# Routing logits with the router weights stationary, and scores and combine weights transposed on VectorE in 32x32 blocks

## Chip, cores and metric

One Trainium2 chip, one core. The metric is the device time of one launch in microseconds (us). Of the kernel before, three runs were timed: 956.42, 960.41 and 960.45 us, median 960.41 us.

## What is computed

Eight rows of 512 tokens with 128 channels go through three layers, each with a residual: a mixture-of-experts feed-forward layer (FFN) at half weight, a Mamba layer, and the same FFN again with the same weights.

```
x = x + 0.5 * ffn(layernorm(x)); x = x + mamba(layernorm(x)); x = x + 0.5 * ffn(layernorm(x))

logits = x @ router_w.T                      # 16 experts
scores = sigmoid(logits); s = scores + bias
group_score = top_k(s in 4 groups of 4, 2).sum; the best 2 groups stay, others are masked
topk_idx = top_k(masked, 4); tw = scores at topk_idx; tw = tw / tw.sum * 2.5
combine = one_hot(topk_idx) * tw             # tokens x 16, mostly zeros
y[e] = (silu(x @ gate_w[e]) * (x @ up_w[e])) @ down_w[e]
ffn = sum over e of y[e] * combine[:, e]  + the same with 2 shared experts, weight 1
```

Everything is float32. The Mamba layer projects, runs a short convolution and a GELU, forms delta, B and C, and scans 16 states per channel over 512 steps.

## The kernel before

The kernel is written for all five engines by hand, in three stages that overlap at their ends: the first FFN (object f1), the Mamba layer, the second FFN (object f2). Each engine has its own generator; the order of instructions on an engine is the order of the yields, and semaphores join the engines.

**The FFN in blocks.** A block is one expert (or one of the 2 shared ones, which come first) of one row of 512 tokens: 18 blocks a row, 144 a layer, numbered g. The float32 products are made of three single-pass products of rounded parts (high x high, low x high, high x low): TensorE issues in each block three matmuls for h (lines L1004, L1005, L1008), three for u (the same lines) and three for the down product of the block four earlier (L986, L987, L988), each 512 columns. ScalarE computes silu(h) (L711, shared experts L701), VectorE multiplies it by the combine weight (L904) and by u (L910), ScalarE rounds the result (L720) and GpSimd subtracts to get the low part (L616). The weight that L904 multiplies by is one expert's combine weight of 512 tokens, the same in all 128 partitions: SyncE loads it from DRAM with a broadcasting DMA into one of 8 slots of `c_ring` (L575). For the first two experts of f1's row 0, TensorE spreads it into PSUM instead (`pe_spread_first`, L971).

**Routing.** For rows in pairs (in f1 rows 0 and 1 singly) the work goes: normalised x is transposed by TensorE (L489) and copied to `xt` (L632); TensorE forms the logits (`pe_logits`, L953), with the tokens of a tile as the stationary operand and the router's 16 columns as the moving one, so that they land with tokens in partitions; ScalarE makes scores from them (`act_scores`, L644, L647); VectorE selects (`dve_route`, L774 to L850) in 13 pieces, one or two in a block; TensorE transposes the combine weights, four tiles a row (`pe_transpose_comb`, L962), into the PSUM half-bank `misc`; ScalarE copies 16 x 512 out of it (`act_copy_ct`, L654); SyncE stores them to DRAM with one DMA (`store_row`, L566), and loads each expert's row back by broadcast. What happens at which block is in the tables `SLOW` and `QUICK` (the second for f1's rows 2 and 3 alone): the step after a pair's start at which x is normalised, turned, copied, the logits and scores are made, the route's pieces, and the turns and copies of the combine weights.

```python
SLOW = Prep((6, 7), (8, 10), (9, 11), 13, 14, {15 + n: 1 for n in range(13)}, (30, 32), (31, 33))
QUICK = Prep((5, 6), (7, 9), (8, 10), 12, 13, {14 + n: 2 for n in range(7)}, (23, 25), (24, 26))
PAIRED = {2: 9, 4: 37, 6: 73}, {2: 1, 4: 37, 6: 73}
```

f1's row 0 is routed before the first block, its row 1 in the blocks 6 to 13. f2's rows 0 and 1 are routed in the last part of the Mamba stage, between the scans; the tables `FRONT_DVE`, `FRONT_PE` and `FRONT_ACT` say after which pair of states. While row 0 of either layer is routed, many operands of VectorE lie in PSUM (`scratch`).

**The Mamba stage** goes by 64 half-rows ("pairs": two states of a row). TensorE spreads B into PSUM (L1462), VectorE multiplies (L1381) and scans (L1411), GpSimd multiplies by C (L1188), TensorE adds the states up (L1474); at the end of each row it projects with plain float32 matmuls (L1484, L1485) and VectorE adds to x (L1395).

**SyncE's queue** issues in order: x, weights, the small operands of the Mamba layer (L319), then the stores of combine weights and the loads of `c_ring`, each load after its slot is free, and at a row's start after that row's store has landed.

## Time and profile before

| | us |
|---|---|
| profiled execution, its own time | 958.39 |
| its span | 956.7 |
| median of 3 runs (lowest, highest) | 960.41 (956.42, 960.45) |
| TensorE busy | 899.6 |
| VectorE busy | 733.7 |
| GpSimd busy | 644.1 |
| ScalarE busy | 582.3 |

TensorE's mean granted clock is 0.987 of full speed. f1 reaches to about 320 us of the span, the Mamba stage to about 635, f2 to the end. Matmul records overlap (each begins before the last one's end), so what a matmul costs is read from one start to the next.

### The profile page before, as it was taken

The numbers are of one execution on the slowest core, as the hardware profiler recorded it, in microseconds if no ns is written. First come the engines' busy times: TensorE is split into PE (matmuls) and PEld (weight loads), VectorE is DVE, ScalarE is ACT, GpSimd is POOL, SyncE is SP. The second block draws the span as 40 slices with busy tenths as digits, with TensorE's granted clock in tenths as the row PEclk, the third lists the DMA queues.
The fourth block names the chain that finished last, engine by engine and source line by source line (L and its number), as shares of the span: only waits on it lengthen the run. The fifth ranks groups of instructions, "written<-read, shape, count | busy, mean of one in ns | idle before, by whom it ended". The sixth has DMA issues, their size and how long they took to land. (4 is left out here: it accounts for less than half of the span.)

```text
span 956.7 us, 11995 instructions
## 1 busy us (share of the span) xinstructions
PE 899.6 (94%) x3623; PEld 641.1 (67%) x3623; DVE 733.7 (77%) x1223; ACT 582.3 (61%) x1038; POOL 644.1 (67%) x469
## 2 busy tenths in 40 slices
PE   5888999999999999899999978799999999999997
PEld 4566788788876766444445424368878878888885
DVE  4777777876874568999999999956877787695664
ACT  5454565566564677889767785226557556555554
POOL 6556575666654465999999888546667567565665
PEclk9999999999999999999999999799999999999999
DMA  9522232243232223344433443233333225334430
GB/s 253 163 77 96 92 120 93 72 150 113 91 101 84 83 77 101 111 156 154 148 133 127 148 151 114 89 127 115 112 104 128 93 87 158 102 99 128 136 113 13
DMA packets 62001, 110.31 MB, mean 115 GB/s; under 512 B 7400, under 2 KB 19824, under 8 KB 61936
## 3 DMA queue, kind: packets, MB, share of 16 engines
q1 hardware_dynamic: 61936, 109.54, 35.6%
q8 instruction: 29, 0.48, 0.2%
q14 instruction: 36, 0.29, 0.1%
HBM read 106.63 MB, written 2.88 MB: 114 GB/s over the span
## 5 line engine op out<-in xcount | busy, mean ns | idle before, releaser
L616 POOL TENSOR_TENSOR act_lo<-act,act_hi 128x512 fp32r<-128x512 f32 x288 | 375.5, 1305 | 263.4 <-ACT act_hi L720 262.8
L711 ACT ACTIVATE bank<-bank 128x512 f32<-128x512 f32 x254 | 147.7, 582 | 250.6 <-PE bank L1008 235.1
L904 DVE TENSOR_TENSOR sg<-bank,c_ring 128x512 f32<-128x512 f32 x254 | 174.2, 686 | 124.1 <-ACT bank L711 118.3
L1004 PE MATMUL bank<-x_parts,w_hi 128*128 128x512 f32 x576 | 241.6, 419 | 14.2 <-DVE act L910 12.5
L910 DVE TENSOR_TENSOR act<-sg,bank 128x512 f32<-128x512 f32 x288 | 198.1, 688 | 59.5 <-PE bank L1008 29.7
L1008 PE MATMUL bank<-x_parts,w_hi 128*128 128x512 f32 x576 | 229.3, 398 | 0.0
L1005 PE MATMUL bank<-x_parts,w_lo 128*128 128x512 f32 x576 | 229.1, 398 | 0.0
L720 ACT ACTIVATE act_hi<-act 128x512 fp32r<-128x512 f32 x288 | 179.4, 623 | 1.7 <-DVE act L910 1.0
L1004 PEld LDWEIGHTS bank<-x_parts,w_hi 128*128 128x128 f32 x576 | 109.7, 191 | 51.0 <-DVE act L910 22.8
L1008 PEld LDWEIGHTS bank<-x_parts,w_hi 128*128 128x128 f32 x576 | 109.6, 190 | 25.9
L1005 PEld LDWEIGHTS bank<-x_parts,w_lo 128*128 128x128 f32 x576 | 110.2, 191 | 24.1 <-issue 2.6
L986 PE MATMUL bank<-act_hi,w_hi 128*128 128x512 f32 x288 | 115.0, 399 | 2.6 <-POOL act_lo L616 2.6
L1275 ACT ACTIVATE stage<-delta,a_neg 128x511 f32<-128x511 f32 x128 | 83.5, 711 | 55.2 <-POOL delta L1158 35.1
L988 PE MATMUL bank<-act_lo,w_hi 128*128 128x512 f32 x288 | 114.0, 396 | 0.0
L987 PE MATMUL bank<-act_hi,w_lo 128*128 128x512 f32 x288 | 113.7, 395 | 0.0
L1188 POOL TENSOR_TENSOR stage<-stage,c_ring 128x1024 f32<-128x1024 f32 x32 | 75.5, 2366 | 14.9 <-DVE stage L1411 14.8
L1188 POOL TENSOR_TENSOR states<-states,c_ring 128x1024 f32<-128x1024 f32 x32 | 75.7, 2367 | 11.9 <-DVE states L1411 11.9
L1381 DVE TENSOR_TENSOR bank<-du,bank 128x1024 f32<-128x1024 f32 x64 | 77.2, 1207 | 3.7 <-PE bank L1462 3.5
L1411 DVE TENSOR_TENSOR_SCAN states<-stage,bank 128x1024 f32<-128x1024 f32 x32 | 73.1, 2283 | 2.2
L1411 DVE TENSOR_TENSOR_SCAN stage<-stage,bank 128x1024 f32<-128x1024 f32 x32 | 72.9, 2278 | 1.1
L1462 PE MATMUL bank<-bc_parts,sel_n 128*128 128x512 f32 x128 | 56.0, 519 | 14.2 <-DVE stage L1411 10.8
L1474 PE MATMUL bank<-states,ident 128*128 128x512 f32 x128 | 63.8, 624 | 4.1 <-DVE y_sb L1389 4.1
(173 smaller groups left out, 1056.4 us busy)
## 6 DMA issues: line engine op xcount, KB each, us to landing
c_ring<-c_dram SPq DMA_DIRECT2D x254, 256.0 KB, 3.2
c_ring<-c_dram SPq DMA_DIRECT2D x64, 512.0 KB, 3.7
out<-x_sb SPq DMA_DIRECT2D x8, 256.0 KB, 2.6
stage<-in_L_ffn_gate_w SPq DMA_DIRECT2D x4, 256.0 KB, 4.9
stage<-in_L_ffn_up_w SPq DMA_DIRECT2D x4, 256.0 KB, 5.1
stage<-in_L_ffn_down_w SPq DMA_DIRECT2D x4, 256.0 KB, 5.2
c_dram<-c_rows SPq DMA_DIRECT2D x24, 32.0 KB, 3.2
x_sb<-in_L_attn_hidden_states SPq DMA_DIRECT2D x2, 256.0 KB, 2.9
```

The costliest lines, as they stand in the source:

```text
L616: self.nc.gpsimd.tensor_tensor(m["act_lo"][:, g % LAG], m["act"][:, g % ACTS], m["act_hi"][:, g % LAG].bitcast(FP32), ALU.subtract).then_i ...
L711: nc.scalar.activation(self.s_bank[:, g % 2], self.h_bank[:, g % 2], ACT.Silu).then_inc(self.sg_ready, 1)
L720: nc.scalar.activation(m["act_hi"][:, j % LAG], m["act"][:, j % ACTS], ACT.Copy).then_inc(self.hi_ready, 1)
L904: nc.vector.tensor_tensor(m["sg"][:, g % 2], silu, weight, ALU.mult).then_inc(self.w_done, 1)
L910: nc.vector.tensor_tensor(m["act"][:, g % ACTS], m["sg"][:, g % 2], self.u_bank[:, g % 2], ALU.mult).then_inc(self.act_ready, 1)
L986: nc.tensor.matmul(self.acc, hi, m["act_hi"][:, j % LAG], start=first, stop=False, skip_group_check=True)
L988: nc.tensor.matmul(self.acc, hi, m["act_lo"][:, j % LAG], start=False, stop=last, skip_group_check=True).then_inc(self.down_done, 1)
L1004: nc.tensor.matmul(dst, m["w_hi"][:, k, n, :], x_hi, start=True, stop=False)
L1005: nc.tensor.matmul(dst, m["w_lo"][:, k, n, :], x_hi, start=False, stop=False)
L1008: return nc.tensor.matmul(dst, m["w_hi"][:, k, n, :], x_lo, start=False, stop=True)
L1188: nc.gpsimd.tensor_tensor(self.state(g), self.state(g), m["c_ring"][:, 2 * (n % RING):2 * (n % RING) + 2], ALU.mult).then_inc(self.mul_don ...
L1411: nc.vector.tensor_tensor_scan(flat(self.state(g)), flat(self.decay[:, g % RING]), flat(self.b_bank[g % 2][:]), 0.0, ALU.mult, ALU.add).th ...
```

## The change

1. The router's weights become the stationary operand (padded with zeros to 32 columns) and 128 tokens the moving one. Each of a row's four tiles of tokens goes to its own 32 partitions of PSUM, which is its own group of 32 columns of TensorE's array. The logits land with experts in partitions: tile t in partitions 32t to 32t+15.
2. ScalarE's two score operations run over 128 x 256 for a pair of rows, not 128 x 128, and write `score_rows` in SBUF.
3. VectorE transposes that in 32x32 blocks into `score` (or the PSUM scratch for row 0), where each tile has 32 places of which 16 are used; and at the end of the route, in a piece of its own, it transposes `comb` (now 32 wide, zeroed at the start) into `c_rows`.
4. TensorE's transposes of the combine weights and ScalarE's copies of them are gone.
5. `c_rows` has tile t in partitions 32t to 32t+15, so a row is stored by four DMAs of 16 x 128, not one of 16 x 512. The Mamba stage gets its own buffer `bc_rows`, and two waits that kept the shared one apart are gone.
6. The first spread reads the new layout: 8 matmuls of 128 columns with 128 partitions, in place of 2 of 512 with 16, one block earlier.

Each object's operations for the parts 1 to 5, cut to the core:

```diff
-FRONT_DVE = {41: 1, 43: 1, 45: 1, 54: 2, 55: 2, 56: 2, 57: 2, 58: 2, 59: 1, 60: 1, 61: 1}
+FRONT_DVE = {41: 1, 43: 1, 45: 1, 54: 2, 55: 2, 56: 2, 57: 2, 58: 2, 59: 1, 60: 1, 61: 1, 62: 1}
-FRONT_ACT = (46, 48, 50, 52, 54, 56, 62)
-FRONT_PE = (49, 51, 52, 61)
+FRONT_ACT = (46, 48, 50, 52, 54, 56)
+FRONT_PE = (49, 51, 52)
-SLOW = Prep((6, 7), (8, 10), (9, 11), 13, 14, {15 + n: 1 for n in range(13)}, (30, 32), (31, 33))
-QUICK = Prep((5, 6), (7, 9), (8, 10), 12, 13, {14 + n: 2 for n in range(7)}, (23, 25), (24, 26))
+SLOW = Prep((6, 7), (8, 10), (9, 11), 13, 14, {15 + n: 1 for n in range(14)})
+QUICK = Prep((5, 6), (7, 9), (8, 10), 12, 13, {14 + n: 2 for n in range(7)})
...
         def store_row(r):
-            sp.wait_ge(self.ct_copied, r + 1)
-            sp.dma_start(self.c_dram[r], m["c_rows"][0:E, r % 2, :]).then_inc(self.ct_stored, 16)
+            sp.wait_ge(self.ct_turned, r + 1)
+            for t in range(TT):
+                sp.dma_start(c_parts[r, t], m["c_rows"][t * Q:t * Q + E, r % 2]).then_inc(self.ct_stored, 16)
...
-    def act_copy_ct(self, ae, r):
...
         dve.wait_ge(self.score_ready, b + 1)
+        cols = slice(P * (r % 2), P * (r % 2 + rows))
+        nc.vector.transpose(turned.rearrange("p t e -> p (t e)"), m["score_rows"][:].rearrange("p r k -> p (r k)")[:, cols]
+                            ).then_inc(self.turned, 1)
+        dve.wait_ge(self.turned, b + 1)
...
+        yield
+        dve.wait_ge(self.comb_ready, b + 1)
+        for n in range(r, r + rows):
+            need(dve, self.ct_stored, self.STORED * (n - 1))
+            nc.vector.transpose(m["c_rows"][:, n % 2], m["comb"][:, TT * (n % 2):TT * (n % 2 + 1)].rearrange(
+                "p t e -> p (t e)")).then_inc(self.ct_turned, 1)
         yield
...
                 if self.p == 0 and 6 <= g < 14:
                     next(routing, None)
-                    if g < 10:
+                    if g < 11:
                         next(routing, None)
...
         for n in range(rows * TT):
-            q, t = (r + n // TT) % 2, n % TT
-            last = nc.tensor.matmul(self.misc[:, n * E:(n + 1) * E], m["xt"][:, q, t * P:(t + 1) * P],
-                                    m["router_sb"][:, :], start=True, stop=True)
+            q, t = n // TT, n % TT
+            last = nc.tensor.matmul(self.misc[t * Q:(t + 1) * Q, q * P:(q + 1) * P], m["router_sb"][:, :],
+                                    m["xt"][:, (r + q) % 2, t * P:(t + 1) * P], start=True, stop=True)
...
-    def pe_transpose_comb(self, pe, r):
```

On TensorE, in f2 at the turn of row 2's combine weights (L962 is that group of four; L988 and L1004 are the block's matmuls around it). Before:

```order
L986 MATMUL bank<-act_hi,w_hi 128x512
L987 MATMUL bank<-act_hi,w_lo 128x512
L988 MATMUL bank<-act_lo,w_hi 128x512
L962 MATMUL bank<-ident,comb 16x128 x4
L1004 MATMUL bank<-x_parts,w_hi 128x512
L1005 MATMUL bank<-x_parts,w_lo 128x512
```

Changed, the same place (the lines have moved up by one):

```order
L985 MATMUL bank<-act_hi,w_hi 128x512
L986 MATMUL bank<-act_hi,w_lo 128x512
L987 MATMUL bank<-act_lo,w_hi 128x512
L1003 MATMUL bank<-x_parts,w_hi 128x512
L1004 MATMUL bank<-x_parts,w_lo 128x512
```

The group of four is gone there and at the other 15 rows of the two layers; the group of logits stays where it was (`L953 ... 128x16 x8` has become `L958 ... 32x128 x8`).

On VectorE, at the end of the Mamba stage, the last three scans (L1411, in the changed kernel L1400; L850 and L849 write the combine weights). Before:

```order
L850 SCALAR_TENSOR_TENSOR comb<-bank,total 128x128
L1411 SCALAR_TENSOR_TENSOR stage<-stage,bank 128x1024
L1381 TENSOR_TENSOR bank<-du,bank 128x1024
L1411 SCALAR_TENSOR_TENSOR stage<-stage,bank 128x1024
L910 TENSOR_TENSOR act<-sg,bank 128x512 x2
```

Changed:

```order
L849 SCALAR_TENSOR_TENSOR comb<-bank,total 128x8x16
L1400 SCALAR_TENSOR_TENSOR stage<-stage,bank 128x1024
L1370 TENSOR_TENSOR bank<-du,bank 128x1024
L856 STREAM_TRANSPOSE c_rows<-comb 128x128 x2
L1400 SCALAR_TENSOR_TENSOR stage<-stage,bank 128x1024
L915 TENSOR_TENSOR act<-sg,bank 128x512 x2
```

Two transposes now stand ahead of the stage's last scan.

On SyncE's queue, at f1's row 0, before and changed:

```order
L319 DMA a_log_sb<-in_L_attn_A_log 128x16
L566 DMA c_dram<-c_rows 16x512
L575 DMA c_ring<-c_dram 128x512 x14
L566 DMA c_dram<-c_rows 16x512
L575 DMA c_ring<-c_dram 128x512 x16
```

```order
L322 DMA a_log_sb<-in_L_attn_A_log 128x16
L575 DMA c_dram<-c_rows 16x128 x4
L584 DMA c_ring<-c_dram 128x512 x14
L575 DMA c_dram<-c_rows 16x128 x4
L584 DMA c_ring<-c_dram 128x512 x16
```

Each store of a row is four issues in place of one, and stands at the same place among the loads.

## Rows read from the trace of the kernel before

**Rows 1.** The page's first part: busy time by engine.
```profile
PE 899.6 (94%) x3623; PEld 641.1 (67%) x3623; DVE 733.7 (77%) x1223; ACT 582.3 (61%) x1038; POOL 644.1 (67%) x469
```
**Rows 2.** Stages: length, busy time of PE, PEld, DVE, ACT, POOL, clock, DMA.
```profile
31.30:60.00 28.70, 21.79 (x83) 15.60 (x84) 27.35 (x68) 12.25 (x20) 16.60 (x12) 0.94 0.33 108
...
84.00:108.00 24.00, 19.48 (x75) 14.47 (x74) 22.79 (x48) 9.86 (x18) 14.70 (x15) 0.93 0.15 47
108.00:240.00 132.00, 132.00 (x609) 106.95 (x607) 95.00 (x189) 79.44 (x154) 83.89 (x66) 1.00 0.34 113
...
582.00:624.00 42.00, 32.73 (x83) 15.44 (x82) 41.40 (x58) 13.34 (x21) 27.38 (x14) 0.84 0.30 107
...
640.00:945.00 305.00, 305.00 (x1377) 247.17 (x1376) 221.59 (x416) 178.84 (x335) 194.55 (x153) 1.00 0.35 111
```
**Rows 3.** Timeline of PE, f1: a turn of combine weights (start, length).
```profile
112.54 0.40 PE L988 MATMUL bank<-act_lo,w_hi 128*128 128x512 f32 x1
112.77 0.60 PE L962 MATMUL bank<-ident,comb 128*16 128x128 f32 x4
113.13 0.48 PE L1004 MATMUL bank<-x_parts,w_hi 128*128 128x512 f32 x1
113.44 0.39 PE L1005 MATMUL bank<-x_parts,w_lo 128*128 128x512 f32 x1
```
**Rows 4.** Timeline of PE, f2: a pair's logits.
```profile
663.73 1.85 PE L953 MATMUL bank<-router_sb,xt 128*128 128x16 f32 x16
665.43 0.48 PE L1004 MATMUL bank<-x_parts,w_hi 128*128 128x512 f32 x1
665.75 0.39 PE L1005 MATMUL bank<-x_parts,w_lo 128*128 128x512 f32 x1
```
**Rows 5.** Timeline of PE, Mamba stage: float32 matmuls of 128 moving columns.
```profile
612.37 0.38 PE L1484 MATMUL bank<-w_out_sb,y_sb 128*128 128x128 f32 x2
612.59 0.39 PE L1485 MATMUL bank<-w_out_sb,z 128*128 128x128 f32 x2
```
**Rows 6.** Groups of DVE by form: busy us, mean ns of one, idle before.
```profile
L787 DVE TENSOR_REDUCE g_score<-pair_sum 128x32 f32<-128x192 f32 x7 | 2.4, 349 | 0.1
...
L803 DVE TENSOR_REDUCE g_rank<-g_ge 128x32 f32<-128x128 f32 x6 | 1.7, 280 | 0.0
...
L774 DVE TENSOR_TENSOR biased<-score,bias_sb 128x64 f32<-128x64 f32 x1 | 1.2, 1232 | 0.0
...
L774 DVE TENSOR_TENSOR biased<-bank,bias_sb 128x64 f32<-128x64 f32 x1 | 0.2, 209 | 0.0
```
**Rows 7.** Timeline of SP, f1's first store and the loads behind it.
```profile
25.56 0.43 SPq L319 DMA_DIRECT2D a_log_sb<-in_L_attn_A_log  x1
26.03 0.43 SPq L566 DMA_DIRECT2D c_dram<-c_rows  x1
28.05 1.28 SPq L575 DMA_DIRECT2D c_ring<-c_dram  x3
```
**Rows 8.** Timeline of DVE, f1: the first product with a loaded weight.
```profile
31.27 0.69 DVE L904 TENSOR_TENSOR sg<-bank,c_ring 128x512 f32<-128x512 f32 x1 [4.46 <-DMA c_ring<-c_dram]
```
**Rows 9.** Timeline of PE, f1: the turn of row 1's combine weights.
```profile
59.38 0.60 PE L962 MATMUL bank<-ident,comb 128*16 128x128 f32 x4 [0.57 <-DVE comb L850]
```
**Rows 10.** Timeline of DVE and POOL, Mamba stage: after the logits, and the last scan.
```profile
581.31 1.23 DVE L1381 TENSOR_TENSOR bank<-du,bank 128x1024 f32<-128x1024 f32 x1 [1.53 <-PE bank L1462]
...
621.05 2.35 POOL L1188 TENSOR_TENSOR stage<-stage,c_ring 128x1024 f32<-128x1024 f32 x1 [1.99 <-DVE stage L1411]
...
622.12 2.29 DVE L1411 TENSOR_TENSOR_SCAN stage<-stage,bank 128x1024 f32<-128x1024 f32 x1
```
**Rows 11.** Waits from 640 to 920 us: total us, times, longest.
```profile
PEld bank L1004 <- DVE act L910: 1.6, 6, 0.3
```

More of the change, by code:

```diff
@@ L16 @@
 TT = SEQ // P
+Q = 32
 E, NSH = 16, 2
@@ L103, in program @@
         c2_dram = nc.dram_tensor("c2_dram", (BATCH, NS, SEQ), FP32, kind="Internal").ap()
-        th = sb("th", [P, 2 * TT, E])
-        score = sb("score", [P, 2 * TT, E])
+        th = sb("th", [P, 2, P])
+        score_rows = sb("score_rows", [P, 2, P])
+        score = sb("score", [P, 2 * TT, Q])
         biased = sb("biased", [P, 2 * TT, E])
@@ L490, in pe_transpose @@
         last.then_inc(self.xt_ready, 1)
-Prep = namedtuple("Prep", "apply turn copy logits scores route comb_turn comb_copy")
-SLOW = Prep((6, 7), (8, 10), (9, 11), 13, 14, {15 + n: 1 for n in range(13)}, (30, 32), (31, 33))
-QUICK = Prep((5, 6), (7, 9), (8, 10), 12, 13, {14 + n: 2 for n in range(7)}, (23, 25), (24, 26))
+Prep = namedtuple("Prep", "apply turn copy logits scores route")
+SLOW = Prep((6, 7), (8, 10), (9, 11), 13, 14, {15 + n: 1 for n in range(14)})
+QUICK = Prep((5, 6), (7, 9), (8, 10), 12, 13, {14 + n: 2 for n in range(7)})
 class Ffn:
     FIRST_STEPS, ROUTE_STEPS = 27, 25
+    STORED = 16 * P // Q
     PAIRED = {2: 9, 4: 37, 6: 73}, {2: 1, 4: 37, 6: 73}
@@ L758, in dve_route @@
         g_rank, g_in = m["g_rank"][:, 0:nt * GROUPS], m["g_in"][:, 0:nt * GROUPS]
-        score, comb = self.route_score(r, rows), m["comb"][:, tiles]
+        turned, comb = self.route_score(r, rows), m["comb"][:, tiles, 0:E]
+        score = turned[:, :, 0:E]
+        g_rank = g_rank.rearrange("p (t g) -> p t g", t=nt)
         if r == 0:
             part = lambda n: self.scratch[:, n * nt * E:(n + 1) * nt * E].rearrange("p (t e) -> p t e", t=nt)
-            rest = lambda n: self.scratch[:, 3 * nt * E:3 * nt * E + nt * n]
-            biased_too = masked = part(1)
-            g_ge = part(2).rearrange("p t (g h) -> p t g h", g=GROUPS)
-            tied = part(2)
-            g_rank, total_too = rest(GROUPS), self.scratch[:, 2 * nt * E:2 * nt * E + nt]
-            g_score_too, n_above, weighted = rest(GROUPS).rearrange("p (t g) -> p t g", t=nt), rest(1), part(3)
+            biased_too = masked = weighted = part(2)
+            g_ge = part(3).rearrange("p t (g h) -> p t g h", g=GROUPS)
+            tied = part(3)
+            total_too = self.scratch[:, 3 * nt * E:3 * nt * E + nt]
+            g_score_too = g_rank = turned[:, :, E:E + GROUPS]
+            n_above = turned[:, :, E]
         else:
@@ L951, in pe_logits @@
         for n in range(rows * TT):
-            q, t = (r + n // TT) % 2, n % TT
-            last = nc.tensor.matmul(self.misc[:, n * E:(n + 1) * E], m["xt"][:, q, t * P:(t + 1) * P],
-                                    m["router_sb"][:, :], start=True, stop=True)
+            q, t = n // TT, n % TT
+            last = nc.tensor.matmul(self.misc[t * Q:(t + 1) * Q, q * P:(q + 1) * P], m["router_sb"][:, :],
+                                    m["xt"][:, (r + q) % 2, t * P:(t + 1) * P], start=True, stop=True)
         last.then_inc(self.logits_ready, 1)
-    def pe_transpose_comb(self, pe, r):
-        nc, m = self.nc, self.m
-        self.onto_misc(pe, self.ct_copied, r + 1)
-        pe.wait_ge(self.comb_ready, self.rows_before(r) + 1)
-        for t in range(TT):
-            last = nc.tensor.transpose(self.misc[0:E, t * P:(t + 1) * P], m["comb"][:, TT * (r % 2) + t, :],
-                                       m["ident"][:, :])
-        last.then_inc(self.ct_ready, 1)
     def pe_spread_first(self, pe):
         self.onto_misc(pe, self.w_done, 1)
-        pe.wait_ge(self.ct_copied, 1)
+        pe.wait_ge(self.ct_turned, 1)
         for e, dst in enumerate((self.misc, self.acc)):
-            self.nc.tensor.matmul(dst, self.m["ident"][0:E, e:e + 1].broadcast_to([E, P]),
-                                  self.m["c_rows"][0:E, 0, :], start=True, stop=True).then_inc(self.spread_ready, 1)
+            for t in range(TT):
+                last = self.nc.tensor.matmul(dst[:, t * P:(t + 1) * P],
+                                             self.m["ident"][:, t * Q + e:t * Q + e + 1].broadcast_to([P, P]),
+                                             self.m["c_rows"][:, 0], start=True, stop=True)
+            last.then_inc(self.spread_ready, 1)
     def pe_down(self, pe, j):
```

67 lines of the change are left out of this document (23 added, 44 removed).

## The prediction, made before the changed kernel was run

> **What bounds the kernel now.** I read the page's busy times first [rows 1]: TensorE is busy for 94% of the span, no other engine above 77%. Such a share is a mean over stages, so I read the table by stage next [rows 2], and it splits the kernel in two kinds of ground. In f2 from 640 to 945 us, and in f1 from 108 to 240 us, TensorE is busy for every microsecond: there each thing taken off its queue shortens the run, and VectorE, busy for about 72% of the time, has room. In f1 from 31 to 60 and from 84 to 108 us, and at the end of the Mamba stage, 582 to 624 us, VectorE is busy for 95% or more and TensorE waits: there TensorE's savings are worth nothing, and each thing put on VectorE lengthens the run. The change takes from TensorE and gives to VectorE, so its parts have to be sorted by stage. The timelines then give the price of each. The sum below is made against the profiled execution's 958.39 us; that is 2.0 us under the median of 960.41, so I put the same difference on the median.
>
> **TensorE: turns of combine weights.** A group of four transposes stands between a block's last down matmul and the next h [rows 3]. Without it, L1004 would start 0.23 us after L988 at 112.77, and L1005 0.23 us later at 113.00; it starts at 113.44. So a group costs 0.44 us, of which about 0.09 is that the matmul behind it starts its successor late (0.31, not 0.23, from 113.13 to 113.44). There are 16 groups. Two are ahead of or at the first blocks of a layer where TensorE waits for others anyway (row 0 of each), f2's row 1 is followed by a wait for VectorE, and f1's row 1 lies in VectorE's stretch. The other 12 lie on TensorE's full ground: 12 x 0.44 = **5.3 us off**.
>
> **TensorE: logits.** The 8 matmuls of a pair are 16 half-products, and the group costs, counted the same way, 665.75 - 663.73 - 0.23 = 1.79 us [rows 4]; 16 x 0.106 and 0.09 behind. Now each moves 128 columns, not 16. The nearest row is the Mamba stage's float32 projection, 128 moving columns: two halves from 612.37 to 612.59, 0.11 us each [rows 5]. No row of the trace shows matmuls on different column groups, so the price must be bounded. If they run one behind the other, 16 x 0.11 + 0.09 = 1.85: nothing gained. If all four tiles of a row run side by side, 4 x 0.11 + 0.09 = 0.53. I take what lies between, for a reason in the order: the two halves of one matmul stand next to each other and use the same column group, so they must follow each other; a half can run beside the next tile's first half only. That gives 9 steps in place of 16: 9 x 0.11 + 0.09 = 1.08. Changing the array from one partition to four and back I charge with 0.2 a group, twice the 0.09 to 0.1 that the trace shows behind a switch between float32 and rounded matmuls [rows 3, 4]. That leaves 1.79 - 1.28 = 0.5 us gained a group, with -0.3 (serial, 1.85 + 0.2) and +1.1 (0.53 + 0.2) as ends. On full ground there are 6 groups, three in each layer; the seventh, for f2's first pair, has VectorE waiting 1.53 us behind it for a spread matmul queued after the logits [rows 10], so it counts too: 7 x 0.5 = **3.5 us off**, ends +1.8 and -7.4.
> The Trainium skill (TensorE: Matmul & The Clock Gate, Part 3) says that matmuls on different column groups start about 4 ns apart, and (TensorEngine Tiling, Key Properties) that changing the tiling mode drains the engine. By the first alone the time would be the side-by-side case; the second speaks against the change and would take some of it back. No row here shows either.
>
> **VectorE: transposes.** 9 for scores, 16 for combine weights. Each reads one SBUF tensor and has no row; the nearest are reductions with one input: 128 elements 280 ns, 192 elements 349 ns [rows 6], so 0.28 for 128 and 0.42 for 256. Where TensorE is full they cost nothing, as long as VectorE does not fall behind by more than it is ahead: between 640 and 920 us TensorE's weight loads waited for it for 1.6 us in six places [rows 11], and the transposes come one or two to a block of 2.1 us in which VectorE is busy for 1.5. If that cover were gone, six pairs times 0.98 us (0.42 + 2 x 0.28) would be exposed. Where VectorE is the bound:
> - 31 to 60 us, row 1's route: 0.28 + 0.28 = 0.56 more. In return TensorE no longer stops at the turn of row 1's weights, for which it waits 0.57 us [rows 9] and then spends 0.44. The acts behind it are as late as VectorE, so I count back only the 0.44: **+0.1** (ends -0.5 and +0.6).
> - 84 to 108 us, rows 2 and 3 at two pieces a block: 0.42 + 0.56, **+1.0**.
> - the Mamba stage's end: 0.42 before the first piece, 0.56 directly ahead of the last scan at 622.12 [rows 10], which GpSimd, the last sums and f2's first block wait for: **+1.0**.
> ScalarE's 16 copies (out of a queue busy 61%) and its two wider score operations change nothing; they have idle time beside them at all places. What follows the transposes in SyncE's queue is now ready sooner than before, except at f2's start, where the first loaded weight is used 15 us later.
>
> **SyncE: four stores for one.** Each issue takes 0.47 us from one start to the next [rows 7]. In the steady part the stores stand well ahead of their use and nothing waits. At f1's row 0 they do not: SyncE is busy with small operands up to 26.03, the loads of `c_ring` start when the store has landed at 28.05, and VectorE waits 4.46 us for the first of them [rows 8], with TensorE behind it. Three more issues put all of that back: 3 x 0.47 = **+1.4**. All else at f1's start (the spread a block earlier, row 0's route 0.56 longer) ends before that load and is hidden by this wait.
>
> **Sum.** -5.3 - 3.5 + 0.1 + 1.0 + 1.0 + 1.4 = -5.3 us: 953.1 against the profiled execution, **955.1 us** against the median. About 0.5%, 4.8 us, is what a measurement of this kernel can tell from no change.
>
> **Rivals.**
> - *Column groups one behind the other.* For it: the names say only where results land, and no row shows an overlap of float32 halves. Then the logits lose 0.3 a group: -5.3 + 1.8 + 3.5 = 0.0, 960.4 us. The whole of the change is then the transposes against VectorE and SyncE. In this case the logits group would cost about 2.0 us in the profile.
> - *All four tiles side by side.* -5.3 - 7.4 + 3.5 = -9.2, 951.2 us. Against it: the halves of a tile are neighbours in the queue.
> - *The transposes wait for GpSimd (slower).* The trace has VectorE operations that last 1.23 us, not 0.21, when both inputs are in SBUF [rows 6]: they start while GpSimd works. If the transposes are held in the same way, each costs up to 1.0 us more in f1's two VectorE stretches (5 of them) and up to 2.35 - 0.28 = 2.1 us in the Mamba stage, where GpSimd's operation of 2.35 us starts at 621.05, just when the two new ones stand ahead of the last scan [rows 10] (3 of them). -5.3 + 5.0 + 6.3 = +6.0: 966.4 us. It ends slower than before from 10.1 us of such waiting upward (5.3 to cancel the gain and 4.8 over it), some 90% of what is possible. Against it: reductions, with one input, show no such spread. The Trainium skill (SBUF — State Buffer, Who interferes with whom) says that only VectorE instructions with two SBUF inputs or in a two-port mode contend with GpSimd; by that rule this rival falls, and the rows of the reductions agree.
> - *A dearer switch.* If draining costs 0.5 us more a group than charged, 3.5 us come back: 958.6.
>
> **Chances.** The forecast's case, column groups that overlap in part and free transposes: 0.47, with some 1.5 us on either side. Serial groups (with the dearer switch): 0.26. Side by side: 0.14. Held transposes, wholly or in part: 0.10. Something not seen: 0.03. The forecast lies just beyond the 0.5% bound, so a little over half of its case, 0.27, counts as faster; with side by side and a rest, 0.44. Within 0.5%: the other 0.20, 0.21 of serial, a little of held transposes, 0.43. Slower: 0.13, most of it from the held transposes and the rest from a switch or a drain dearer than the trace can show. The range takes in the three cases without the held transposes' end, and the bounds of the small terms: 950.0 to 962.5.
>
> **What would show it.** The gap that the logits leave on TensorE, from the group's start to the second matmul behind it: 1.5 us in the forecast (0.23 more than the group's cost), 2.3 serial, 1.0 side by side. L1004 straight behind L988 at the old turns. Transposes of 0.28 and 0.42 us, with no long ones. VectorE's wait for the first `c_ring` load grown, and that load landing 1.4 us later; the last scan 1 us later against the start of the route. If f2's full stretch, first h of row 1 to last down product, is not 4 us shorter (6 turns x 0.44 + 3 x 0.5), the TensorE half is wrong; if it is and the total is not, the price was paid in f1.

## The result, and the profile after

The changed kernel takes **947.49 us** (median of 4 runs, 945.70 to 948.37) against 960.12 for the kernel before (4 runs, 956.42 to 960.45). The ratio is 0.988 with a 95% interval of 0.9855 to 0.9905: faster by 1.2%, some 12.6 us. The forecast was 955.1, the range 950.0 to 962.5: the time lies below the range, past even the rival with the best end (all tiles side by side, 951.2). The profiled execution took 948.37 us, span 946.5, against 958.39 and 956.7 before.

The page's first part, as [rows 1], and the table by stage, as [rows 2]; the stages from the Mamba layer's end on now start 6 us earlier (start and end in the first column, the length behind them, then as in [rows 2]).

```profile
PE 885.0 (93%) x3571; PEld 622.9 (66%) x3571; DVE 735.2 (78%) x1249; ACT 576.4 (61%) x1022; POOL 643.6 (68%) x470
```

```profile
34.00:62.00 28.00, 22.16 (x77) 16.16 (x78) 26.27 (x68) 12.16 (x20) 15.11 (x11) 0.88 0.36 113
86.00:108.00 22.00, 18.39 (x73) 12.90 (x72) 20.74 (x49) 9.15 (x16) 14.78 (x16) 1.00 0.17 50
108.00:240.00 132.00, 132.00 (x607) 105.31 (x606) 98.31 (x199) 79.92 (x153) 85.40 (x68) 1.00 0.37 113
576.00:618.00 42.00, 32.04 (x101) 15.20 (x101) 40.67 (x59) 12.95 (x20) 26.80 (x14) 0.92 0.31 100
634.00:935.00 301.00, 301.00 (x1355) 240.89 (x1354) 223.97 (x429) 177.02 (x330) 195.33 (x154) 1.00 0.36 112
```

The kinds of ground are the same: TensorE still full in f2 and late f1, VectorE still the bound in the two early stretches and at the Mamba stage's end. VectorE's total rose by 1.5 us only (733.7 to 735.2) although the 25 transposes bring 7.7 us of work: some of its old work became shorter. That is the first hint of what the forecast missed.

Where the time went is best read between fixed points: the start of ScalarE's silu of a block, and of VectorE's last long scan. Differences of the two profiled executions, with what the forecast's own terms put into each stretch:

| Stretch | before | after | difference | forecast |
|---|---|---|---|---|
| span's start to f1 block 6 | 32.05 | 35.10 | +3.05 | +1.4 |
| f1 block 6 to 36 (both VectorE stretches, 1 logits, 2 turns of pairs) | 84.14 | 79.52 | -4.62 | -0.3 |
| f1 block 36 to 110 (2 logits, 4 turns) | 167.08 | 163.92 | -3.16 | -2.8 |
| f1 block 110 to the last scan | 338.85 | 340.61 | +1.76 | +0.5 |
| last scan to f2 block 3 | 17.22 | 14.69 | -2.53 | 0 |
| f2 block 3 to 143 (3 logits, 6 turns) | 306.48 | 301.84 | -4.64 | -4.1 |
| sum | | | -10.14 | -5.3 |

**Logits.** TensorE's timeline at the place of [rows 4], then at that of [rows 3] (start, length).

```profile
658.09 0.39 PE L987 MATMUL bank<-act_lo,w_hi 128*128 128x512 f32 x1
658.41 0.64 PE L958 MATMUL bank<-xt,router_sb 128*32 128x128 f32 x16
658.99 0.50 PE L1003 MATMUL bank<-x_parts,w_hi 128*128 128x512 f32 x1
659.32 0.40 PE L1004 MATMUL bank<-x_parts,w_lo 128*128 128x512 f32 x1
```

```profile
111.39 0.39 PE L987 MATMUL bank<-act_lo,w_hi 128*128 128x512 f32 x1
111.62 0.40 PE L1003 MATMUL bank<-x_parts,w_hi 128*128 128x512 f32 x1
111.86 0.39 PE L1004 MATMUL bank<-x_parts,w_lo 128*128 128x512 f32 x1
```

From L987 to L1004 it is 1.23 us with the logits between, and 0.47 without: a group of logits costs 0.76 us, where it cost 1.78 counted the same way. That is 1.02 gained a group, twice the 0.5 of the forecast. The single records show why: the sixteen halves start in four rounds of four, 0.11 to 0.13 us from round to round and 6 to 7 ns from one half to the next within a round. From the group's start to the second matmul behind it the gap is 0.91: of the three markers (1.5, 2.3, 1.0) the side-by-side one. The turn has left no trace: L1003 stands straight behind L987.

**The start of f1.** Timeline of SyncE, then of VectorE, as [rows 7] and [rows 8].

```profile
26.04 0.43 SPq L322 DMA_DIRECT2D a_log_sb<-in_L_attn_A_log  x1
26.51 1.82 SPq L575 DMA_DIRECT2D c_dram<-c_rows  x4
30.80 0.34 SPq L584 DMA_DIRECT2D c_ring<-c_dram  x1
```

```profile
34.31 0.69 DVE L909 TENSOR_TENSOR sg<-bank,c_ring 128x512 f32<-128x512 f32 x1 [7.87 <-DMA c_ring<-c_dram]
```

From the first store's issue to the first load's it is now 4.29 us, before 2.02: 1.4 of the growth are the three more issues, 0.9 is that the last of the four took 2.87 us from issue to landing (the first three 1.75 to 1.87), the single one 2.00. With the queue 0.48 us later already at the store (26.51, not 26.03) and the load itself 0.29 us slower (30.80 to 34.31, before 28.05 to 31.27), VectorE's wait ends 3.04 us later.

**The transposes.** VectorE's groups by form.

```profile
L856 DVE STREAM_TRANSPOSE c_rows<-comb 128x128 f32<-128x128 f32 x16 | 4.1, 290 | 0.1
L771 DVE STREAM_TRANSPOSE score<-score_rows 128x256 f32<-128x256 f32 x6 | 2.6, 438 | 0.0
...
L771 DVE STREAM_TRANSPOSE score<-score_rows 128x128 f32<-128x128 f32 x1 | 0.3, 303 | 0.0
```

0.29 and 0.44 us against 0.28 and 0.42 estimated. The longest of all 25 took 0.45, though 23 of them ran, at least in part, while a GpSimd operation did: the slower rival, transposes held by GpSimd, is out. (The rule cited for it, the Trainium skill, SBUF — State Buffer, Who interferes with whom, agrees.)

### The profile page after: what moved, and what is told of

It is laid out like the page before. It is cut to its first block and busy times, and to the rows that moved or that the text cites. A ratio compares the mean times of both kernels' runs of the same rounds, so it can differ in the third digit from the quotient of the medians.

```text
span 946.5 us, 11926 instructions
## 1 busy us (share of the span) xinstructions
PE 885.0 (93%) x3571; PEld 622.9 (66%) x3571; DVE 735.2 (78%) x1249; ACT 576.4 (61%) x1022; POOL 643.6 (68%) x470
## 5 line engine op out<-in xcount | busy, mean ns | idle before, releaser
L1003 PE MATMUL bank<-x_parts,w_hi 128*128 128x512 f32 x576 | 240.3, 417 | 19.6 <-DVE act L915 16.0
L1004 PE MATMUL bank<-x_parts,w_lo 128*128 128x512 f32 x576 | 229.2, 398 | 0.0
L1003 PEld LDWEIGHTS bank<-x_parts,w_hi 128*128 128x128 f32 x576 | 109.1, 189 | 59.1 <-DVE act L915 26.5
L1004 PEld LDWEIGHTS bank<-x_parts,w_lo 128*128 128x128 f32 x576 | 109.3, 190 | 25.2 <-issue 2.6
L987 PE MATMUL bank<-act_lo,w_hi 128*128 128x512 f32 x288 | 114.3, 397 | 0.0
L1400 DVE TENSOR_TENSOR_SCAN states<-stage,bank 128x1024 f32<-128x1024 f32 x32 | 73.0, 2282 | 3.9 <-PE bank L1463 1.9
L1400 DVE TENSOR_TENSOR_SCAN stage<-stage,bank 128x1024 f32<-128x1024 f32 x32 | 72.9, 2278 | 1.0
L1463 PE MATMUL bank<-states,ident 128*128 128x512 f32 x128 | 66.7, 648 | 4.6 <-DVE y_sb L1378 4.6
```

Source lines behind the costliest of these rows:

```text
L1003: nc.tensor.matmul(dst, m["w_hi"][:, k, n, :], x_hi, start=True, stop=False)
L1004: nc.tensor.matmul(dst, m["w_lo"][:, k, n, :], x_hi, start=False, stop=False)
L1400: nc.vector.tensor_tensor_scan(flat(self.state(g)), flat(self.decay[:, g % RING]), flat(self.b_bank[g % 2][:]), 0.0, ALU.mult, ALU.add).th ...
```

## The experiments

Twelve kernels ran, four at a time on one chip with the kernel before. The intervals are those of the ratio to it; its median was 960.10 us beside the first four, 960.59 beside the second four, and 958.79 beside the last four, which ran on another chip. So times of the last four are compared with the others' by their ratios. "f1's block 6 to 36" and the like are stretches read as in the table above.

### The changed kernel again

> The changed kernel once more, unchanged, as the yardstick of this series and for a second trace. If what happened in the first layer's VectorE-bound stretches belongs to the program, the block of f1 that comes 3.05 us late at g = 6 comes 3 us late again, and the lead at the second layer's start is again about 5 us. If it was the luck of one execution, these two numbers move by 1 us or more. Time 947.5.

**947.00 us**, ratio 0.9867 (0.984 to 0.9895). Block 6 of f1 came at 35.10 again, exactly; block 36 at 114.52 (114.62 in the first trace). The lead at f2's first block was 7.3 us, where the first trace had 5.8: f1's block 110 to the last scan took 339.27, not 340.61. So in these two executions the start and f1's lengths repeat, and the Mamba stage scatters. In four traces of kernels that leave this stage as it was before, it takes 338.85, 342.97, 341.09 and 340.16 us. The first of these is that of the kernel before: its profiled execution had the shortest Mamba stage of all, which is part of why the profiled executions differ by 10.0 us and the medians by 12.6.

### One column group, two column groups

```diff
-            last = nc.tensor.matmul(self.misc[t * Q:(t + 1) * Q, q * P:(q + 1) * P], ...
+            last = nc.tensor.matmul(self.misc[0:Q, q * P:(q + 1) * P], ...
```

> All tiles of tokens put their logits on the first column group, one over the other (so the scores are those of the last tile of a row, and three quarters of the score rows hold what was there before). Same instructions, same sizes, only the column group differs. Theory A, the four groups run side by side: on one group the 16 halves follow each other at 0.11 us, a group of logits costs about 1.9 us instead of 0.77, and on the six groups that TensorE's queue decides this gives 6 x 1.1 = 6.7 us back: about 954. Theory B, a matmul with 32 stationary columns is cheap by itself, wherever its result lands: the gap stays at 1.0 us from the group's start to the second matmul behind it, and the time at 947.5.

```diff
+            last = nc.tensor.matmul(self.misc[(t % 2) * Q:(t % 2 + 1) * Q, q * P:(q + 1) * P], ...
```

> Tiles alternate between the first two column groups (the scores of two of the four tiles are overwritten, half of the score rows hold what was there before). Theory A, neighbours on different groups overlap: eight steps of 0.11 instead of about four, a group of logits costs 1.2 to 1.3 us, the time is about 950.5. If instead two halves of one matmul must follow each other and only neighbours overlap (the forecast's reason), two groups are as good as four, and the time stays at 947.5. Theory B: 947.5 as well, so this run counts together with the one on a single group.

One group: **956.52 us**, ratio 0.996 (0.9943 to 0.9977). Two groups: **950.59**, ratio 0.9904 (0.9877 to 0.9931). Timelines of TensorE at the same logits of f2, first with one group, then with two.

```profile
661.83 0.39 PE L987 MATMUL bank<-act_lo,w_hi 128*128 128x512 f32 x1
662.15 1.93 PE L958 MATMUL bank<-xt,router_sb 128*32 128x128 f32 x16
664.01 0.51 PE L1003 MATMUL bank<-x_parts,w_hi 128*128 128x512 f32 x1
664.36 0.39 PE L1004 MATMUL bank<-x_parts,w_lo 128*128 128x512 f32 x1
```

```profile
659.76 0.39 PE L987 MATMUL bank<-act_lo,w_hi 128*128 128x512 f32 x1
660.08 1.07 PE L958 MATMUL bank<-xt,router_sb 128*32 128x128 f32 x16
661.08 0.51 PE L1003 MATMUL bank<-x_parts,w_hi 128*128 128x512 f32 x1
661.42 0.39 PE L1004 MATMUL bank<-x_parts,w_lo 128*128 128x512 f32 x1
```

Counted as above (L987 to L1004 less 0.47) a group costs 2.06 us with one column group, 1.19 with two, 0.76 with four. The three lie on a line: one group to two saves 0.87 = 8 x 0.109, two to four saves 0.43 = 4 x 0.108. So the 16 halves go in 16, 8 and 4 rounds of 0.11 us, and 0.33 us is left over that does not depend on the groups. The forecast had charged 0.29 for the change of the array's shape and the slower start behind it; that these are what the 0.33 pays for fits, but no run changes the shape alone. Theory A is shown, and the forecast's reason is not only weakened but excluded: if two halves of one matmul held up the queue, two groups would be as good as four. The single-group kernel also confirms the serial case of the forecast, 1.85 + 0.2 = 2.05 a group. Its time is 9.5 us over that of the changed kernel beside it, where 6.7 was expected: 7 x 1.30 = 9.1, which fits all seven groups counting, the one in the Mamba stage too. (The Trainium skill, TensorE: Matmul & The Clock Gate, Part 3, has it that matmuls on different column groups start about 4 ns apart. The traces agree in kind: the halves of four tiles start 6 to 7 ns apart and run at the same time, in float32 too.)

### The turns alone

Router and scores as before, the combine weights turned by VectorE and stored four times. The old logits put tokens on other partitions than the turn by blocks assumes, so the weights belong to other tokens of the row; amount and order of the work are those described.

```diff
-            last = nc.tensor.matmul(self.misc[t * Q:(t + 1) * Q, q * P:(q + 1) * P], m["router_sb"][:, :],
-                                    m["xt"][:, (r + q) % 2, t * P:(t + 1) * P], start=True, stop=True)
+            last = nc.tensor.matmul(self.misc[:, n * E:(n + 1) * E], m["xt"][:, (r + q) % 2, t * P:(t + 1) * P],
+                                    m["router_sb"][:, 0:E], start=True, stop=True)
...
-        nc.vector.transpose(turned.rearrange("p t e -> p (t e)"), ...
```

> The combine weights turned by VectorE as in the change, with the four stores, but logits and scores as before: tokens stationary, 16 moving columns, no transpose of scores. If the logits' part is worth 6 x 1.0 us on TensorE's full ground and its extra transposes cost nothing, this run is 6 us slower than the changed kernel: 953.5. If the better VectorE stretches of f1 came with the logits' part, it is slower still, 955 to 957. The late start must show in both cases: block g = 6 of f1 about 3 us late, since the stores are in it.

**954.30 us**, ratio 0.995 (0.9928 to 0.9973): the turns, with the late start that they bring, are worth 5.8 us, the logits with their scores the other 7.3, near to 7 x 1.02. In f1's blocks 18 to 24, where one group of logits stands, this kernel takes 15.26 us, the changed one 14.24: there too the whole 1.02 is gained. Each turn takes 0.40 to 0.43 us out of f2's blocks (forecast 0.44), and block 6 of f1 is late by 3.19 us: the late start is in the stores, as expected.

### GpSimd's subtraction cut short, in both kernels

```diff
+                w = 8 if self.p == 0 and 5 <= g < 60 else SEQ
-                self.nc.gpsimd.tensor_tensor(m["act_lo"][:, g % LAG], m["act"][:, g % ACTS], ...
+                self.nc.gpsimd.tensor_tensor(m["act_lo"][:, g % LAG, 0:w], m["act"][:, g % ACTS, 0:w], ...
```

> The kernel before, with GpSimd's subtraction act_lo cut from 512 to 8 columns in f1's blocks 5 to 59 (the low part of these acts is then stale, so the output is off in the last bits). Theory A, f1's VectorE-bound stretches are long because small VectorE operations with two inputs wait for this 1.29 us subtraction: before has ten such operations there, 6.5 to 9 us more than they need, so this kernel is 5 to 9 us faster than the kernel before, 951 to 955, and without long small operations in the two stretches. Theory B, the collisions are hidden by other waits: no more than 1 us faster.

> The same cut in the changed kernel. Theory A, the change was better than forecast in f1's VectorE stretches only because it met GpSimd less often there (2.1 us of it in two operations of rows 2 and 3): with the collisions gone in both kernels, block 28 of f1 relative to before is no longer 4.7 us (3.7 without the logits' gain) ahead of where block 6 stood, but behind by the transposes' own time, about 1 us, less the gains of TensorE; after gains only 3 to 5 us from the cut, and the gap between the kernels closes from 13 to 9 or 10 us. Theory B, the gain there comes from TensorE's turns being gone: the gap stays at 13.

What is suspected, in the rows. Kernel before, timeline of VectorE and under it of GpSimd, 88 to 99 us (an operation's start and length):

```profile
88.52 1.43 DVE L800 TENSOR_TENSOR g_ge<-g_ge,g_gt 128x128 f32<-128x128 f32 x1
...
97.62 1.42 DVE L831 TENSOR_TENSOR tie_at<-tie_at,n_above 128x128 f32<-128x128 f32 x1
```

```profile
88.51 1.29 POOL L616 TENSOR_TENSOR act_lo<-act,act_hi 128x512 fp32r<-128x512 f32 x1 [0.33 <-ACT act_hi L720]
...
97.59 1.29 POOL L616 TENSOR_TENSOR act_lo<-act,act_hi 128x512 fp32r<-128x512 f32 x1 [2.58 <-ACT act_hi L720]
```

The changed kernel, the same two operations and the GpSimd subtraction beside them:

```profile
89.51 0.29 DVE L800 TENSOR_TENSOR g_ge<-g_ge,g_gt 128x128 f32<-128x128 f32 x1
98.11 0.29 DVE L831 TENSOR_TENSOR tie_at<-tie_at,n_above 128x128 f32<-128x128 f32 x1
```

```profile
89.53 1.43 POOL L625 TENSOR_TENSOR act_lo<-act,act_hi 128x512 fp32r<-128x512 f32 x1 [0.33 <-ACT act_hi L718]
...
98.61 1.29 POOL L625 TENSOR_TENSOR act_lo<-act,act_hi 128x512 fp32r<-128x512 f32 x1 [0.81 <-ACT act_hi L718]
```

Before, VectorE's L800 starts 0.01 us behind GpSimd's subtraction and needs 1.43 us; after, it starts 0.02 us ahead of it, needs 0.29, and GpSimd's takes 1.43 in place of 1.29. Who comes second waits, and if that is a VectorE operation of 0.3 us, it waits for up to 1.15. The kernel before has ten small VectorE operations of routes and norm drawn out to 0.8 us or more in the two stretches, 11.6 us together; the changed one has six, 6.6 us together.

Measured: the kernel before with the cut **952.12 us**, ratio 0.992 (0.9899 to 0.994), the changed one with the cut **942.66**, ratio 0.982 (0.9789 to 0.985). Against 960.59 and the changed kernel's 947.49, the cut gains 8.5 us in the kernel before and 4.8 in the changed one, and the gap closes from 13.1 to 9.5. The cut also ends GpSimd's own work sooner, but TensorE waited only once for that work in f1's block 6 to 36 before, 0.2 us, and not at all in the changed kernel: what is gained is the collisions. In the traces f1's block 6 to 36 falls from 84.14 to 76.43 before, and from 79.52 to 74.44 after: without most collisions (two long operations are left before, one after) the change gains 1.99 us in this stretch, with them 4.62. Theory A holds; in these traces 2.6 us of the result are collisions that fell better. Which part of the change moved VectorE against GpSimd so (the late start, the transposes, the turns gone from TensorE) is not separated.

The other traces say where this is luck. L800 and L831 in f1's blocks 24 to 36 are held in the trace of the kernel before and in that of the same kernel with the early store (33.06 and 33.13 us for these blocks), and not in that of the kernel before shifted by 64 bytes (31.11; both kernels come below). All traces with the change and the full subtraction take 30.45 to 30.50 there but one, the combined kernel: it holds both again and takes 32.31. So three quarters of the gain in blocks 24 to 36 (1.95 of 2.57 us) hang on an order of events that small changes undo.

### The start: one store, and an early store

One store of all 128 partitions a row, in place of four:

```diff
-            for t in range(TT):
-                sp.dma_start(c_parts[r, t], m["c_rows"][t * Q:t * Q + E, r % 2]).then_inc(self.ct_stored, 16)
+            sp.dma_start(c_parts[r], m["c_rows"][:, r % 2]).then_inc(self.ct_stored, 16)
```

> A row's weights stored with one DMA from all 128 partitions (rows of unused experts too, into a DRAM tensor twice as tall) in place of four. Theory A, the late start is the three more issues on SyncE, 0.47 us each: the first load of a weight is issued 1.4 us sooner than in the changed kernel (29.4 instead of 30.80) and VectorE's first weighted product, at 34.31 there, comes at 32.9; the time is 946 or, if the collisions fall as in the changed kernel, up to 1.4 us under it. Theory B, it is the landing of the store in small rows of 512 bytes and the slow first load: the product comes within 0.5 us of 34.3. Theory C, the late start is hidden later on in any case, since another resource sets block 12 and on: the product comes sooner, and the time stays at 947.5.

Four stores, but in another place of SyncE's queue:

```diff
         store_row(0)
+        if self.p == 0:
+            self.setup.load_small(sp, 5)
         for r in range(BATCH):
...
+                if self.p == 0 and r == 0 and e == C_SLOTS - 1:
+                    self.setup.load_small(sp, 12)
```

> The changed kernel with row 0's four stores and the first six loads of weights moved ahead of most small operands in SyncE's queue: store straight behind the load of W_in (the turned weights are ready at 20.2 us, the queue is free at 20.7), five small loads while it lands, six loads of weights, then the other seven small ones. The loads should start at about 25.3 instead of 30.8 and VectorE's first weighted product come at about 29 instead of 34.3. If nothing else waits there, all of it is gained: 942 to 943. Rival: the weights of the next experts (loads, ScalarE's high parts, GpSimd's low parts) are the next to be late, or the lead is lost again to collisions as the late start was given back: 945 to 947.5.

One store: **946.11 us**, ratio 0.9859 (0.9827 to 0.989), not to be told from the changed kernel. Its first weighted product comes at 32.31, 2.0 us sooner (1.4 expected), and all blocks of f1 keep 1.94 of it. Between the last scan and f2's block 3 its trace gives 1.5 back, to the clock (below). Its single store landed 2.52 us after its issue, the last of the four 2.87 after its own. So the start is late by Theory A's three issues (1.4 us) and by 0.4 of Theory B's landing, and the time cannot show it.

Early store: **942.79 us**, ratio 0.9821 (0.9791 to 0.9851), as forecast. Timelines of SyncE and VectorE:

```profile
20.52 2.12 SPq L581 DMA_DIRECT2D c_dram<-c_rows  x4
...
25.09 1.27 SPq L592 DMA_DIRECT2D c_ring<-c_dram  x3
```

```profile
30.03 0.69 DVE L919 TENSOR_TENSOR sg<-bank,c_ring 128x512 f32<-128x512 f32 x1 [3.70 <-DMA c_ring<-c_dram]
```

The product comes 4.3 us sooner, a microsecond less than hoped, and every block from 36 of f1 to 143 of f2 is 5.2 us ahead of the changed kernel's. SyncE's queue was the bound of the start. (The first load now takes 4.9 us to its use, not 3.5, which is the missing microsecond.)

### The same order of the queue in the kernel before

> The kernel before with the order of SyncE's queue of the early-store experiment: row 0's store straight behind the load of W_in, the first six loads of weights ahead of most small operands. In before the combine weights reach SBUF later, through TensorE and ScalarE, and the first weighted product stood at 31.27. If this start is gained as in the changed kernel, that product comes at 28 to 29 and the time is 957 to 958; if the collisions of VectorE with GpSimd fall otherwise it may be anything from 955 to 960.5. What the change is worth at an equal start is the difference to 942.8.

**957.02 us**, ratio 0.998 (0.9958 to 1.0003): hardly a gain. There the turned weights go through TensorE and ScalarE and are stored at 22.18, not 20.52; the first weighted product comes at 29.37, 1.9 us sooner than in [rows 8]. Block 36 of f1 is 2.2 us ahead, and its trace loses 1.7 of it around the Mamba stage, where executions scatter. At an equal start the change is worth 957.0 - 942.8 = 14.2 us by the times and 15 by the ratios (0.998 less 0.9821), the two kernels having run on different chips.

### Sixty-four bytes

The table above has an oddity: f2's full stretch gained 4.64 us, though three logits at 1.02 and six turns at 0.42 make 5.6 us. The rest is spread evenly over blocks in which nothing differs.

```diff
-        router_sb = sb("router_sb", [P, Q])
+        sb("router_hole", [P, E])
...
         comb = sb("comb", [P, 2 * TT, Q])
+        router_sb = sb("router_sb", [P, Q])
```

> The changed kernel with only the address of router_sb changed: a hole of the old size stands at its old place and the tensor, 64 bytes wider, is allocated behind comb, so that x_parts, act, act_hi and act_lo lie where they lay before the change. In every trace with the change a plain stretch of f2's blocks, where nothing differs, takes 0.3% longer (blocks 36 to 50: 30.72 us, before 30.60 to 30.61). Theory A, that is the shift of the matmuls' moving operands by 64 bytes: here the stretch is back at 30.61, which over f1's and f2's full ground is 1.5 us: 946. Theory B, it has another cause (more work on VectorE, other tensors' places): 30.72 and 947.5.

```diff
         router_sb = sb("router_sb", [P, E])
+        sb("router_hole", [P, E])
```

> The kernel before with a hole of 64 bytes behind router_sb, so that all later tensors lie 64 bytes further on, and nothing else. Theory A: f2's blocks 36 to 50 take 30.72 us in place of 30.60, and the time is 1.5 us over that of before, some 961.5. Theory B: 30.60 and no difference.

Timeline of ScalarE, the silu of f2's blocks 36 and 50: the kernel before, then before shifted by 64 bytes, then the changed kernel with router_sb at the end.

```profile
711.82 0.60 ACT L701 ACTIVATE sg<-bank 128x512 f32<-128x512 f32 x1 [0.97 <-PE bank L1008]
...
742.43 0.58 ACT L711 ACTIVATE bank<-bank 128x512 f32<-128x512 f32 x1 [0.97 <-PE bank L1008]
```

```profile
712.18 0.60 ACT L702 ACTIVATE sg<-bank 128x512 f32<-128x512 f32 x1 [0.98 <-PE bank L1009]
...
742.91 0.58 ACT L712 ACTIVATE bank<-bank 128x512 f32<-128x512 f32 x1 [0.99 <-PE bank L1009]
```

```profile
703.86 0.60 ACT L702 ACTIVATE sg<-bank 128x512 f32<-128x512 f32 x1 [0.97 <-PE bank L1008]
...
734.47 0.58 ACT L712 ACTIVATE bank<-bank 128x512 f32<-128x512 f32 x1 [0.97 <-PE bank L1008]
```

30.61, 30.73 and 30.61 us: Theory A in both directions for this stretch. In the kernel before, nothing but a hole of 64 bytes makes f2's stretch from block 3 to 143 last 307.52 instead of 306.48; in the changed one, taking the shift away makes it 301.15 instead of 301.84 (not in all of its blocks: blocks 15 to 31 took 34.03 us, against 34.07 with the shift, and 33.96 to 34.03 in traces of the old layout). The times do not show it: router_last **946.64 us**, ratio 0.9874 (0.9844 to 0.9904), where the changed kernel itself had 0.9867 and 0.988; before_shifted **959.81**, ratio 1.001 (0.9992 to 1.0027), 1.0 us over the kernel before beside it, with an interval that takes in both 0 and the 1.5 us expected. In its trace L800 and L831 of the second VectorE stretch missed their collisions and f1's block 6 to 36 was 1.7 us shorter, as much as the shift cost elsewhere. Which of the shifted tensors matters was not tried.

### Combined

Early start, one store a row, router_sb at the end: the three diffs together.

> The changed kernel with the early start, one store a row in place of four, and router_sb allocated behind comb. Theory A (each is worth what it was alone, 4.7 for the early start, one store saves three issues at the start again, and 1.5 for the addresses): 939.5 to 941.5. Theory B: only the early start counts, 942.8.

**941.15 us** (938.69 to 941.97), ratio 0.9817 (0.9787 to 0.9846): faster than both kernels, by the ratios 5 to 6 us under the changed one. The time lies within A's bounds, but it does not decide for A: the early-store kernel had the ratio 0.9821 on its chip, so the two cannot be told apart, and Theory B fits as well. The trace shows why. f1's blocks 36 to 110 and f2's 3 to 143 are 0.6 and 1.2 us shorter than in the early-store kernel, as the addresses should give; but its second VectorE stretch meets GpSimd five times (5.7 us in long operations, 3.1 in the early-store kernel), which takes back most of that.

## Why the prediction was wrong, step by step

The direction was right, the size short by 7.6 us, and the time fell out of the range. With the one step that failed put right the sum gives 951.5 us, inside the range still; the other 4.0 us are terms that were mis-sized or missing.

- **Logits, 7 x 0.5: the step that failed.** The forecast held that "the two halves of one matmul ... must follow each other; a half can run beside the next tile's first half only", which gave nine steps. The halves of one tile do follow each other, but the other tiles' halves do not wait for them: four rounds, not nine. The term should have been 7 x 1.02 = 7.1, 3.6 us more. The side-by-side end of the bounds (0.53 + 0.2 = 0.73) was within 0.03 us of the truth; it got 0.14 of the chance on an argument from order alone.
- **Turns, 12 x 0.44.** Right: 0.40 to 0.43 each. The two at f2's start were costed at nothing. From the last scan to f2's block 3 the traces that keep the old turns and had full clock there take 16.1 and 15.7 us, those with the new turns at full clock 14.7, the turns-alone kernel among them: this ground was worth 1.0 to 1.5 us more.
- **VectorE's stretches, +0.1 and +1.0.** The transposes cost what was said. What the sum missed is that collisions move: the forecast used the rule on GpSimd only to ask whether the new operations would be held, not whether shifting VectorE by 1 to 3 us changes which of the old ones are. Block 6 to 36 gained 4.62 where 0.3 was expected, 2.6 of it by collisions. Of the other 1.99, blocks 18 to 24 gained 1.00 in the two kernels with the cut, the logits; blocks 6 to 18 gained 0.34, where +0.1 was charged, and blocks 24 to 36 gained 0.65, where the transposes' +1.0 less two turns made +0.1. That row 1's turn on TensorE stopped the acts with its wait as well, the -0.5 end, would go the way of the 0.34; it was not tested, and the held operations that are left weigh as much.
- **SyncE, +1.4.** Mis-sized: +3.05 at block 6. The three issues were 1.4, but the last of the four stores also landed later after its issue than the single one (0.9), and the queue came 0.5 later to the store. That last part scatters: block 6 starts at 32.05, 32.59 and 32.94 us in the traces with the old stores, and at 34.63 to 35.73 in the seven with four stores at the old place in the queue, 2.6 us later on average.
- **The Mamba stage, +1.0.** The two executions show +1.76 with the logits' gain in it, but this stretch scatters by 4 us between the four kernels whose code in it is that of before. Their mean is 340.8 us and that of the ten with the new one 340.4, so the term can be neither confirmed nor refuted.
- **Not in the sum at all:** the 64 bytes (0.3 to 0.4% on TensorE's full ground, 1.1 to 1.6 us in f1 and f2 together by the two address kernels), and the clock. Behind its pause at 632 us the kernel before fell to half clock, the changed one behind a like pause did not. The table by windows of TensorE (length, busy, granted clock, DMA), before and after:

```profile
632.00:634.00 2.00, 0.38 (x3) 1.00 0.00 0
634.00:636.00 2.00, 2.00 (x16) 0.77 0.03 8
636.00:638.00 2.00, 2.00 (x7) 0.50 0.00 0
638.00:640.00 2.00, 2.00 (x9) 0.88 0.03 11
```

```profile
627.00:629.00 2.00, 0.35 (x2) 1.00 0.97 344
629.00:631.00 2.00, 1.33 (x12) 1.00 0.44 168
631.00:633.00 2.00, 2.00 (x14) 1.00 0.00 0
```

Two matmuls of the kernel before in the slow window, on TensorE's timeline; four more lie between them:

```profile
636.26 0.63 PE L1005 MATMUL bank<-x_parts,w_lo 128*128 128x512 f32 x1
...
638.40 0.44 PE L1004 MATMUL bank<-x_parts,w_hi 128*128 128x512 f32 x1
```

At 0.50 (1.2 GHz) they start 0.43 us apart, at 1.00 (2.4 GHz) 0.23: five such steps are 1.0 us, and the slow ones ahead of them come on top. The same fall is in one other trace of the four that keep the old turns, and in one of the ten with the new ones (the one-store kernel, 16.18 us from the last scan to f2's block 3, not 14.69). Whether the change makes it rarer is open. A second fall stands in f1: from 92 to 96 us the kernel before runs at 0.59 and 0.56, after TensorE was busy for 0.10 of the 2 us from 90, and the changed one stays at 1.00. Such a fall is in the three traces where L800 was held in this stretch, and in no other. What it cost cannot be read: the two held operations (1.14 and 1.13 us too long) account for all that blocks 24 to 36 take more than in before_shifted (33.06 against 31.11), which has neither.

Against these misses the late start and the 64 bytes worked the other way. That the error is only 0.8% is in part this luck. The two profiled executions differ by 10.0 us only; the rest up to the medians' 12.6 fits the short Mamba stage of the one before, 2.6 us under the mean of the other three.

The marker for f2 ("4 us shorter") was met: 4.64. It was met because the logits' double gain and the 64 bytes partly cancel, so a total over a stretch was a poor test of a term. The marker on the single gap (0.91 us against 1.5, 2.3, 1.0) decided at once.

## What to carry to other kernels

A group of float32 matmuls with 32 stationary columns was paid here in rounds of 0.11 us, one for each matmul half on the fullest column group, plus 0.33 us that did not depend on the groups: spread it over all four. A vector operation that stands where VectorE is the bound has the price of its own duration and of every collision with GpSimd that it moves; before trusting a sum of durations there, list the long outliers and ask which GpSimd operation each one met. And look at what SyncE issues ahead of the first transfer that the blocks wait for: in the changed kernel moving small loads behind it was worth 4.7 us, more than a third of the whole change, and in the kernel before, where the weights are ready later, 1.8 us that its interval does not tell from nothing.

## What the runs showed of the hardware that was not expected

- Four float32 matmuls on four column groups started 6 to 7 ns apart, and the halves on one group followed each other at 0.11 us; no group's halves waited for another's.
- Shifting the tensors behind router_sb, the moving operands of the blocks' matmuls among them, by 64 bytes in SBUF made f2's blocks 36 to 50 0.4% slower (30.73 against 30.61 us for 14 blocks), and taking the shift away brought it back.
- VectorE and GpSimd excluded each other for a whole operation, and 0.01 to 0.02 us of lead decided who waited: the same VectorE operation took 1.43 or 0.29 us. The transposes were not held. Which operations meet changes with small edits ahead of them, and in part from run to run: block 6 to 36 of f1 took 79.52 and 79.42 in two traces of the changed kernel, but of its first three held operations (L783, L797, L800) the second trace has only L800, with L793 and L805 beside it. The stretch takes 78.6 to 80.1 in the kernels with the full change, four groups and the full subtraction, 82.4 to 84.1 in those that keep the old turns and the full subtraction.
- At f1's row 0 the last of four stores of 8 KB landed 2.9 us after its issue, one of 32 KB 2.0 after its own. That belongs to this place: over the whole trace the medians are 1.8 us for the 64 small stores and 1.7 for the 16 large ones.
